# Routed rows that carry the twice-normalised values, with the gate and epsilon folded into two scalars per row

## The reference

```python
x = x + _layernorm(attn(_layernorm(x)))            # causal attention, low-rank keys and values
f = _layernorm(x)
scores = f @ centroids.T
expert = argmax(scores)
alpha = sigmoid(sum(f * centroids[expert]))
mu, var = mean(f), mean((f - mu)**2)
h = (f - mu) * rsqrt(var + EPS) * g + b            # the expert's own layer norm
y = f + relu(h @ W1e.T + b1e) @ W2e.T + b2e
x = x + _layernorm(alpha * y + (1 - alpha) * f)
```

## Time and profile before

| | us |
|---|---|
| median of three runs | 1458.52 |
| lowest and highest run | 1456.14 and 1459.41 |
| span of the profiled execution | 1455.6 |
| PE, DVE, ACT, POOL busy in it | 1391.0, 1244.1, 1092.1, 809.9 |
| attention loop | about 40 to 1240 |
| first tile loaded | 1256.28 |
| last scatter issued | 1446.44 |

### The profile page before, as it was taken

How to read it: one execution, slowest core, us unless ns; L and a number is a source line. 1 busy time by engine, 2 the same in 40 slices (tenths; PEclk the granted TensorE clock), 3 DMA queues, 4 the chain that set the end, 5 groups by cost and what they waited for, 6 DMA issues and landing times.

```text
span 1455.6 us, 37790 instructions
## 1 busy us (share of the span) xinstructions
PE 1391.0 (96%) x10656; PEld 1319.1 (91%) x10656; DVE 1244.1 (85%) x4806; ACT 1092.1 (75%) x3186; POOL 809.9 (56%) x1216
## 2 busy tenths in 40 slices
PE   7999999999999999999999999999999999599993
PEld 6999999999999999999999999999999999488872
DVE  4888898989898989898888989898989887499994
ACT  5888787878787878788787878787878886366661
POOL 3455455555555555555555555555555554178886
PEclk9999999999999999999999999999999999699997
DMA  5000000000000000000000000000000000312120
GB/s 195 5 9 13 12 11 10 10 11 11 12 11 12 11 8 11 12 11 12 11 11 12 11 10 11 10 11 12 11 12 11 9 9 13 96 48 63 58 63 8
DMA packets 38795, 32.42 MB, mean 22 GB/s; under 512 B 4882, under 2 KB 35990, under 8 KB 38304
## 3 DMA queue, kind: packets, MB, share of 16 engines
q1 hardware_dynamic: 31968, 21.61, 4.9%
q0 software_dynamic: 4608, 8.67, 1.7%
q10 hardware_dynamic: 2112, 1.11, 0.3%
HBM read 20.35 MB, written 12.07 MB: 22 GB/s over the span
## 4 chain that ended last, share of the span: by engine, by line
PE 76%; DVE 11%; issue 7%; ACT 2%; POOL 2%; DMA 1%; DVEq 0%; SPq 0%; POOLq 0%; ACTq 0%
PE psS L577 22%; PE psZU L643 11%; PE psP L606 11%; PE psZU L628 11%; PE psZU L631 6%; PE psT L594 4%; PE psT L596 4%; PE psT L595 4%; DVE ff L365 2%; DVE wup_s L382 1%; DVE on L391 1%; DVE nscore L849 1%; POOL out L444 1%; DVE gg L400 1%; DVE p_lo L859 1%
## 5 line engine op out<-in xcount | busy, mean ns | idle before, releaser
L1035 POOL TENSOR_TENSOR prob<-prob,rinv 128x256 f32<-128x256 f32 (+1 forms) x512 | 412.6, 826 | 501.3 <-DVE rinv L830 496.0
L720 ACT ACTIVATE prob<-nscore,nmax 128x128 f32<-128x128 f32 (+1 forms) x1024 | 457.9, 448 | 227.3 <-DVE nmax L849 226.6
L849 DVE CUSTOM_DVE_ANT_0 nscore<-psS,mask 128x128 f32<-128x128 f32 (+1 forms) x1024 | 320.8, 351 | 3.8 <-issue 0.2
L577 PE MATMUL psS<-xt_hi,t_lo 128*128 128x128 f32 (+1 forms) x1024 | 305.5, 298 | 0.0
L577 PE MATMUL psS<-xt_lo,t_hi 128*128 128x128 f32 (+1 forms) x1024 | 284.4, 278 | 0.0
L577 PE MATMUL psS<-xt_hi,t_hi 128*128 128x128 f32 (+1 forms) x1024 | 283.8, 277 | 0.0
L859 DVE TENSOR_TENSOR p_lo<-psP,p_hi 128x768 fp32r<-128x768 f32 x256 | 243.7, 952 | 0.9 <-ACT p_hi L693 0.8
L606 PE MATMUL psP<-ident,prob 128*128 128x128 f32 x1536 | 209.6, 272 | 7.8 <-DVE p_lo L859 7.8
L836 DVE TENSOR_TENSOR t_lo<-psT,t_hi 128x512 fp32r<-128x512 f32 x256 | 175.9, 687 | 44.3 <-ACT t_hi L693 41.6
L693 ACT ACTIVATE p_hi<-psP 128x768 fp32r<-128x768 f32 x256 | 206.1, 805 | 3.3 <-PE psP L606 1.6
L865 DVE TENSOR_TENSOR z_lo<-psZU,z_hi 128x512 fp32r<-128x512 f32 x256 | 176.8, 690 | 31.1 <-ACT z_hi L693 14.6
(11 more groups left out here) (167 smaller groups left out, 3315.4 us busy)
## 6 DMA issues: line engine op xcount, KB each, us to landing
fin<-routed_rows SPq DMA_DIRECT2D x40, 136.0 KB
wx<-ffn_w SPq DMA_DIRECT2D x2, 2058.0 KB, 12.3
xin<-x SPq DMA_DIRECT2D x32, 128.0 KB, 2.1
xres<-x SPq DMA_DIRECT2D x32, 128.0 KB, 2.1
out<-res,fin POOLq DMA_INDIRECT x80
routed_rows<-padr ACTq DMA_DIRECT2D x4, 272.0 KB, 4.8
routed_rows<-padr SPq DMA_DIRECT2D x4, 272.0 KB, 4.2
wup_s<-wup SPq DMA_DIRECT2D x1, 1024.0 KB, 5.0
```

Of the source, the lines that this page charges most:

```text
L577: last = mm(psS[:, h, a:z], tt[:, tb, h, q * P:(q + 1) * P], xx[:, xb, 0:z - a], start=(n == 0), stop=(n == 2))
L720: last = nc.scalar.activation(prob[:, p1, h, a:z], nscore[:, h, a:z], ACT.Exp, bias=nmax[:, p1, h, q:q + 1], scale=-1.0, accum_out=rsum[:, ...
L849: last = v.tensor_tensor_reduce(nscore[:, h, a:z], psS[:, h, a:z], mask[:, a:z], -1.0, -MASKED, ALU.add, ALU.min, nmax[:, p1, h, q:q + 1])
L1035: last = g.tensor_tensor(pr, pr, rinv[:, p2, :, q:q + 1].broadcast_to([P, 2, z - a]), ALU.mult)
```

## The change

The row of `routed_rows` grows from 136 to 260 numbers: x (128), the twice-normalised values nn = fn * rstd2 (128), gain = rstd2 * alpha, eps = rstd2^2 * EPS, and the token number. All of these are made once for each block in the attention loop. nn and eps are made by GpSimd in slot 3 of the block; the exponential of the score by ScalarE at the start of slot 5; the sum with 1 and the reciprocal by VectorE in slot 6; the gain by GpSimd in slot 6. The scatter moves on GpSimd from slot 5 to slot 6, behind the gain. In the expert stage TensorE transposes the loaded columns directly; VectorE's `gg` is branch * gain + nn, and GpSimd's `gve` adds the loaded eps. `ff`, `nn`, `ea` and `alpha` of the expert stage go, and so does the shift. The padding has the same 512 rows per expert, of 260 numbers now, with EPS in their eps column.

```diff
...
-ROW = 136
+C_NN = 128
+C_GAIN = 256
+C_EPS = 257
+C_ID = 258
+ROW = 260
...
                 if live(0):
-                    pe.wait_ge(S["nn_ready"], m0 + s + 1)
+                    pe.wait_ge(f_loaded[s], n0 + 16)
...
-                        last = nc.tensor.transpose(psN[:, t * P:(t + 1) * P], nn[:, t, :], ident[:])
+                        last = nc.tensor.transpose(psN[:, t * P:(t + 1) * P], fin[:, s, t, C_NN:C_NN + P], ident[:])
...
-                    act.wait_ge(f_loaded[s], n0 + 16)
-                    nc.scalar.activation(ea[:, s, :], fin[:, s, :, C_SCORE], ACT.Exp,
-                                         scale=-1.0).then_inc(S["exp_done"], 1)
...
-                        last = v.scalar_tensor_tensor(gg[:, b, t, :], psO[:, t, 0:P], alpha[:, sf, t:t + 1],
-                                                      ff[:, sf, t, :], ALU.mult, ALU.add)
+                        last = v.scalar_tensor_tensor(gg[:, b, t, :], psO[:, t, 0:P], fin[:, sf, t, C_GAIN:C_GAIN + 1],
+                                                      fin[:, sf, t, C_NN:C_NN + P], ALU.mult, ALU.add)
...
-                    g.tensor_tensor(gve[:], gmv[:, b3, :, 1], eps_t[:], ALU.add).then_inc(S["gve_done"], 1)
+                    g.tensor_tensor(gve[:], gmv[:, b3, :, 1], fin[:, sf3, :, C_EPS], ALU.add).then_inc(S["gve_done"], 1)
...
+                if r == 5 and live_b(2):
+                    act.wait_ge(S["argmax_steps"], 4 * (b0 + db) - 7)
+                    nc.scalar.activation(ea[:], best[:], ACT.Exp, scale=-1.0).then_inc(S["exp_done"], 1)
...
+                if r == 6 and live_b(2):
+                    dve.wait_ge(S["alpha_steps"], 2 * (b0 + db) - 3)
+                    v.reciprocal(alpha[:], ea1[:]).then_inc(S["alpha_steps"], 1)
...
-                    v.scalar_tensor_tensor(pay[:, db, :, C_SHIFT], mv3[:, :, 0], -1.0, pay[:, db, :, C_RSTD],
-                                           ALU.mult, ALU.mult)
...
+                if r == 6 and live_b(2):
+
+                    dve.wait_ge(S["exp_done"], b0 + db - 1)
+                    v.tensor_scalar(ea1[:], ea[:], 1.0, None, ALU.add).then_inc(S["alpha_steps"], 1)
...
+            step(g.memset(padr[:, :, C_EPS:C_EPS + 1], EPS))
...
+                if r == 3 and live_b(2):
+
+                    n = b0 + db - 1
+                    pool.wait_ge(S["f_ready"], n)
+                    g.tensor_tensor(pay[:, db, :, C_NN:C_NN + P], fn[:],
+                                    rstd2[:].unsqueeze(2).broadcast_to([P, 2, P]), ALU.mult).then_inc(S["nn_stored"], 1)
+                    g.tensor_tensor(sq2[:], rstd2[:], rstd2[:], ALU.mult).then_inc(S["gain_steps"], 1)
+                    pool.wait_ge(S["gain_steps"], 2 * n - 1)
+                    g.tensor_tensor(pay[:, db, :, C_EPS], sq2[:], eps_t[:], ALU.mult).then_inc(S["gain_steps"], 1)
...
-                if r == 5 and live_b(2):
+                if r == 6 and live_b(2):
+                    n = b0 + db - 1
                     if not live(0) and db == 1:

                         pool.wait_ge(S["pad_stored"], 16 * E)
-                    wait_apart(pool, S["dest_ready"], b0 + db - 1)
+                    pool.wait_ge(S["alpha_steps"], 2 * n)
+                    g.tensor_tensor(pay[:, db, :, C_GAIN], rstd2[:], alpha[:], ALU.mult).then_inc(S["gain_ready"], 1)
+                    wait_apart(pool, S["dest_ready"], n)
+                    pool.wait_ge(S["gain_ready"], n)
+                    pool.wait_ge(S["nn_stored"], n)
...
```

More of the change, by code:

```diff
@@ L124, in block_kernel @@
         ve3 = sb("ve3", [P, 2])
+        rs3 = sb("rs3", [P, 2])
         w3 = sb("w3", [P, 3, 2])
+        rstd2 = sb("rstd2", [P, 2])
+        sq2 = sb("sq2", [P, 2])
+        best = sb("best", [P, 2])
+        ea = sb("ea", [P, 2])
+        ea1 = sb("ea1", [P, 2])
+        alpha = sb("alpha", [P, 2])
         fn = sb("fn", [P, 2, P])
@@ L151, in block_kernel @@
             st3_done mv3_done r3_steps f_ready f_tr ft_ready scored argmax_steps onehot_ready ranked dest_steps
-            dest_ready scattered"""
+            dest_ready scattered nn_stored exp_done alpha_steps gain_steps gain_ready"""
         S = {n: sem(n) for n in names.split()}
@@ L180, in block_kernel @@
         yt = sb("yt", [P, T])
-        ea = sb("ea", [P, FU, 2])
-        ea1 = sb("ea1", [P, 2])
-        alpha = sb("alpha", [P, FU, 2])
         gg = sb("gg", [P, 2, 2, P])
@@ L191, in block_kernel @@
         res = sb("res", [P, 2, 2, P])
-        for n in """pads_ready pad_stored spare_stored ends_ready table_steps table_ready wst_ready exp_done nt_ready
-            relu_a relu_d ff_done nn_ready n_tr h_done yt_done yt_ready y_tr alpha_steps g_steps gmv_ready gve_done
+        for n in """pads_ready pad_stored spare_stored ends_ready table_steps table_ready wst_ready nt_ready
+            relu_a relu_d n_tr h_done yt_done yt_ready y_tr g_steps gmv_ready gve_done
             grs_ready on_ready res_ready""".split():
@@ L361, in slot @@
             def slot(m0, n0, s, live):
-                if live(0):
-                    dve.wait_ge(f_loaded[s], n0 + 16)
-                    for t in range(2):
-                        last = v.tensor_scalar(ff[:, s, t, :], fin[:, s, t, 0:P], fin[:, s, t, C_RSTD:C_RSTD + 1],
-                                               fin[:, s, t, C_SHIFT:C_SHIFT + 1], ALU.mult, ALU.add)
-                    last.then_inc(S["ff_done"], 1)
-                if live(0):
-                    dve.wait_ge(S["ff_done"], m0 + s + 1)
-                    if live(1):
-                        dve.wait_ge(S["n_tr"], m0 + s)
-                    for t in range(2):
-                        last = v.tensor_scalar(nn[:, t, :], ff[:, s, t, :], fin[:, s, t, C_RSTD2:C_RSTD2 + 1], None,
-                                               ALU.mult)
-                    last.then_inc(S["nn_ready"], 1)
                 if live(1):
@@ L407, in slot @@
                     last.then_inc(S["g_steps"], 1)
-                if live(0):
-                    dve.wait_ge(S["exp_done"], m0 + s + 1)
-                    v.tensor_scalar(ea1[:], ea[:, s, :], 1.0, None, ALU.add).then_inc(S["alpha_steps"], 1)
                 if live(3):
@@ L417, in slot @@
                     last.then_inc(S["gmv_ready"], 1)
-                if live(0):
-                    dve.wait_ge(S["alpha_steps"], m0 + s + 1)
-                    v.reciprocal(alpha[:, s, :], ea1[:])
             ffn_phases(dve, slot)
@@ L877, in route @@
                 over = lambda a: a.unsqueeze(2).broadcast_to([P, 2, E])
-                best = pay[:, db, :, C_SCORE]
                 if r == 4:
@@ L882, in route @@
                         dve.wait_ge(S["scored"], n + 1)
-                        v.tensor_reduce(best, scv, AX.X, ALU.max).then_inc(S["argmax_steps"], 1)
+                        v.tensor_reduce(best[:], scv, AX.X, ALU.max).then_inc(S["argmax_steps"], 1)
                     elif k == 1:
                         dve.wait_ge(S["argmax_steps"], 4 * n + 1)
-                        v.tensor_tensor(hits[:], scv, over(best), ALU.is_ge).then_inc(S["argmax_steps"], 1)
+                        v.tensor_tensor(hits[:], scv, over(best[:]), ALU.is_ge).then_inc(S["argmax_steps"], 1)
                     elif k == 2:
@@ L949, in misc @@
                     normalise(lambda t: fn[:, t, :], lambda t: pay[:, db, t, 0:P], mv3,
-                              lambda t: pay[:, db, t, C_RSTD:C_RSTD + 1], S["f_ready"])
+                              lambda t: rs3[:, t:t + 1], S["f_ready"])
                 if r == 2 and live_b(-1):
```

18 lines of the change are left out of this document (5 added, 13 removed).

## The result

The changed kernel takes 1461.49 us (median of ten runs, 1460.97 to 1463.50), the kernel before 1457.60 us beside it. The two medians stand as 1.0027 to 1; the ratio on record, taken over the fast runs alone (one run of the kernel before took 1783 us), is 1.0031 with a 95% interval of 1.0023 to 1.0039: slower by 0.3%, the way of case A. The profiled execution has a span of 1459.2 us against 1455.6.

The account below looks back on a forecast made before the run. GpSimd's own instructions were taken to set the expert stage, TensorE the attention loop. Expert stage 1.7, passage with first tile 1.2, loop 0 and start 0.1 made +3.0 us on 1458.52, so 1461.5; range 1456.5 to 1467.

Parts of the forecast that it names:

- case A: Whole kernel: the terms as summed, +3.0 us, 1461.5 us; chance 0.56.
- expert stage: Steady expert stage: GpSimd's period becomes the tail's 4.28 us in all 39 periods, +1.7 us.
- passage, landing of the scatter, net: Serial passage: last-but-one block's scatter lands 2.6 us later behind wider padding, 1.1 hidden ahead of `ft`; net +1.5 us.
- passage, two VectorE steps: Serial passage: the add on `ea` and the reciprocal now stand between `dst` and `cnt` of the last block, +0.4 us.
- passage, last scatter and table to load: Serial passage: the last scatter starts later and just catches up with the table that releases the load, +0.1 us.
- passage, first load less `ff` and `nn`: Expert stage, first tile: longer rows add 0.4 us to the load, removing `ff` and `nn` saves 1.18 us.
- passage, ramp to the first scatter, and rounding: Expert stage, first tile: the ramp to the first scatter is TensorE's work and unchanged.
- attention loop: Attention loop: TensorE sets the slots and all added work stays off its path, 0 us.
- start: Kernel start: wider fill of `padr` and a small extra fill delay the constants, +0.1 us.
- only direct waiter: Serial passage: only the last block's scatter waits directly for the padding, after 1252, with padding ending near 1249.5.
- 0.3 left: Attention loop, slot 7: `rs2` ends at 729.0 and `an` needs it at 729.28, leaving 0.3 us of cover.
- rival D: Attention loop: less cover than read, before `an`, at the landing wait or slot 5's copy; total about +7.5, 1466; chance 0.13.

Follow-up runs that it names:

- Experiment one: Changed kernel with two VectorE statistics instructions of 128 columns put ahead of `on` in the expert stage: 1468.54 us (ratio 1.0078).
- experiment three: `gve`, then `gve` and `res`, moved from GpSimd to VectorE: changed kernel 1452.08, then 1445.72 us; kernel before 1457.74, then 1453.22 us.
- experiment five: Changed kernel, GpSimd's scatter-landing wait in the last two blocks dropped: 1469.91 us; replaced by a wait for something long done: 1460.39 us.

## Why the prediction was right, step by step

| term, us | predicted | measured |
|---|---|---|
| expert stage | +1.7 | +1.72 |
| passage, landing of the scatter, net | +1.5 | +1.40 |
| passage, two VectorE steps | +0.4 | +0.15 |
| passage, last scatter and table to load | +0.1 | +0.24 |
| passage, first load less `ff` and `nn` | -0.8 | -0.76 |
| passage, ramp to the first scatter, and rounding | 0 | +0.13 |
| attention loop | 0 | +0.65 |
| start | +0.1 | 0 |
| sum | +3.0 | +3.5 (span: +3.6) |

**Expert stage: right, and for the reason given.** The tail of the earlier trace rows showed the period that GpSimd keeps when VectorE waits for it, 4.28 us, and it became the period of most tiles. That the term came out to the hundredth is luck: I set 4.28 for all 39 periods against a mean of 4.24 that holds one of 4.96 and one of 3.99, and seven tiles kept 4.22. Experiment one took the 0.06 us per scatter away and got 1.65 of the 1.72 us back. The temptation in the earlier trace rows, VectorE at 98%, was wrong twice over: GpSimd set the pace, and part of that 98% was VectorE being held by GpSimd (experiment three).

**The landing: the net right, its parts off.** The slip of `pay` was put at 2.6 us and was 3.22. Of this, 0.65 came with the whole attention loop, 0.70 from the later start of the scatter (the handover between GpSimd's own gain and its scatter takes 0.88 us, where I had 0.3, although shows 0.85 for the same handover behind `res`), and 1.87 from the queue. The cover ahead of `ft` was 1.2 us, 1.1 predicted. The rule that I cited from the Trainium skill (DMA: Bandwidth & Descriptors, "Queues, rings and completion order") gave a slip of about 1.5 us, and my own reckoning by order in the queue 2.5 without the later start: the queue's 1.87 lies between them, nearer to the rule. My reckoning also has an error in it: 46 ns for a packet is not halfway between 29 and the 55 of bytes alone. Halfway is 42, which gives 2.0. With the rates measured, 292 and 337 GB/s while the engines are full (1238 to 1244 before, 1238 to 1250 after), a packet takes 30 and 49 ns, and by order in the queue the slip would be about 2.9, an estimate from these rates. The padding stream lasted till about 1251 and not 1249.5: the engines went from 281 to 353 GB/s in the microsecond that I had looked at, but from the first issue to the last full microsecond it took 14.5 us, in place of 9.2 before. Its "only direct waiter" had 1.4 us to spare, and experiment five showed how soon it counts.

**Two VectorE steps: too dear.** I had 0.2 us for each. The sum with 1 stands before `cnt` without waiting for `dst`, and both together cost 0.15.

**Last scatter and table: 0.24 where I had 0.1.** The last scatter now lands at 1258.56, behind the table and 0.15 us ahead of the load; the load follows the end of the table by 1.04 us in place of 0.80.

**First load: right.** From issue to TensorE's start 1261.40 - 1258.71 = 2.69 us; before, 2.27 to the start of `ff`. +0.42 for the longer row, as taken. (The 2.24 of the prediction is a misreading of this 2.27.)

**Attention loop: the step that failed.** "0.3 left" before `an` was too much, because of the handover again: 0.91 us and not 0.3.

```profile
724.93 1.08 POOL L1070 DMA_INDIRECT routed_rows<-pay,dst  x1 [0.91 <-POOL pay L1065]
726.32 0.96 POOL L1070 DMA_INDIRECT routed_rows<-pay,dst  x1 [0.30 <-issue]
727.30 1.62 POOL L1020 TENSOR_TENSOR prob<-prob,rinv 128x256 f32<-128x256 f32 x2
```

`prob` of slot 7 starts at 727.30, not 726.4, and `an` at 729.90 right behind `rs`. In the blocks inside a turn `an` is 0.24 us later, but the next turn gives all but 0.05 of it back, so rival D did not come by that way. From the first to the last turn it is 907.3 us before, 908.0 after, 907.5 with the replaced wait, whose loop is the changed kernel's, and 908.3 with only the row widened, whose loop is that of before. By these sums the differences between equal loops are as large as the one to be explained.

Slot by slot, from the starts of TensorE's `psT` in one profile of each kernel, they come apart. The slot with the branch takes 4.5 to 4.9 us in every kernel that has not lost the 8 us; its sum over 13 turns is 60.0 to 61.3 us without the change and 59.7 to 60.4 with it, so it differs from run to run and not with the change. The other 195 slots take 922.8 us in the three kernels with the old row (before, and the two with GpSimd's work moved), 923.3 with only the row widened, and 923.5 to 923.6 in all six that have the change and not the loss. So about 0.7 us is a price of the change, and 0.4 of it came with the wide row alone. It is spread over TensorE's slots in steps of some 6 ns that no recorded wait explains, and its cause stays open. "All of it is off TensorE's path, so 0" was therefore wrong by this 0.7. It is not known to come from the missing cover ahead of `an`: no slot there shows a step of more than 0.02 us.

**The range.** 1456.5 to 1467.0 held the result; slower by over 0.2% had a chance of 0.50, and it came out there by a tenth of a per cent. That the median met 1461.5 to a hundredth is luck. The forecast was 1458.52 + 3.0; the kernel before measured 1457.60 in ten runs, 0.9 us under the median of three, and the shift of the medians was 3.9 us, 0.9 more than the sum. As a ratio the forecast is 1.0020, just under the measured interval.

## What to carry to other kernels

A high busy share shows neither the bound nor the room: look for the engine that waits for nobody, and for a stretch (a tail) where the rival engine is idle, since it shows the pace after the rival's work is gone. Taking work from an engine that doesn't set the pace pays only when the pacing engine's work can then be moved to it; here the first alone cost 0.3%, and both together gained 0.8%. When a wait moves, list what is next in time on the same resource: behind the landing of one scatter stood the padding stream, 1.4 us away.

## What the runs showed of the hardware that I had not expected

- GpSimd's own write to its own indirect scatter: 0.88 to 0.91 us from the end of a 128x2 product to the start of the scatter that reads it, and 0.85 us behind `res` at the last tile, against 0.2 to 0.3 us ahead of a scatter whose inputs are long written.
- A VectorE instruction held by GpSimd shows as a longer busy one and not as a wait: a sum with 1 over 256 numbers takes 0.15 us alone and 0.46 us when it starts during a GpSimd scatter; a product of 256 numbers takes 0.16 us alone and 0.62 us when it starts together with a GpSimd product.
- Under the same queues the 16 DMA engines moved 292 GB/s with rows of 544 bytes and 337 GB/s with rows of 1,040 bytes, over the stretch in which they were full.
- At each turn of the attention loop VectorE stood for 2.3 to 2.7 us on "issue", in all kernels looked at. With one wait fewer behind the loop, 0.7 us came on top in the slot ahead, 8 us over 13 turns, twice as much as the change itself.
